# x copied into the output in DRAM, relu results added there by accumulating transfers, in a graph-attention layer kernel

## The reference

```python
h = jnp.maximum(_layernorm(x, axis=-1), 0.0)
q = jnp.einsum('c,bcn->bn', wq, h)
k = jnp.einsum('c,bcn->bn', wk, h)
scores = q[:, None, :] + k[:, :, None]
scores = jnp.where(scores > 0, scores, 0.01 * scores)
att = jax.nn.softmax(scores, axis=-1)
agg = jnp.einsum('bcn,bmn->bcm', h, att)
out = jnp.einsum('oc,bcm->bom', adj, agg) + bm[None, :, None]
x = x + jax.nn.relu(out)
```

## Time and profile before

| | us |
|---|---|
| median of 3 runs | 2090.09 |
| lowest, highest | 2087.72, 2090.14 |
| the profiled execution | 2090.47 |
| its span from first to last instruction | 2088.7 |
| PE busy | 2051.5 (98%) |
| DVE busy | 1674.8 (80%) |
| ACT busy | 1221.5 (58%) |
| POOL busy | 379.6 (18%) |
| DMA queue of SP, share of 16 engines | 37.1% |

### The profile page before, as it was taken

How to read it: one execution, slowest core, us unless ns; L and a number is a source line. 1 busy time by engine, 2 the same in 40 slices (tenths; PEclk the granted TensorE clock), 3 DMA queues, 4 the chain that set the end, 5 groups by cost and what they waited for, 6 DMA issues and landing times.

```text
span 2088.7 us, 33534 instructions
## 1 busy us (share of the span) xinstructions
PE 2051.5 (98%) x10448; PEld 950.3 (45%) x10448; DVE 1674.8 (80%) x3661; ACT 1221.5 (58%) x1871; POOL 379.6 (18%) x273
## 2 busy tenths in 40 slices
PE   5899999999999999999999999999999999999999
PEld 2344444444444444444444444444444444444444
DVE  7978878778887788887788877888877888778853
ACT  5556656556655566565566555665655665556634
POOL 1012211112111122111121111221111211112212
PEclk9999999999999999999999999999999999999999
DMA  5244433344324444333433234442334432343332
GB/s 195 64 155 142 148 99 123 138 160 141 133 84 136 151 141 146 104 118 137 161 141 133 84 136 151 141 146 105 117 137 161 141 131 86 136 152 141 106 101 76
DMA packets 126395, 271.46 MB, mean 130 GB/s; under 512 B 22624, under 2 KB 23136, under 8 KB 122208
## 3 DMA queue, kind: packets, MB, share of 16 engines
q1 hardware_dynamic: 123904, 269.01, 37.1%
q10 hardware_dynamic: 2400, 1.58, 0.3%
HBM read 202.91 MB, written 67.63 MB: 130 GB/s over the span
## 4 chain that ended last, share of the span: by engine, by line
PE 95%; DVE 3%; DMA 1%; POOL 0%; issue 0%; ACT 0%; POOLq 0%; SPq 0%; DVEq 0%
PE mix L385 21%; PE mix L387 21%; PE mix L386 21%; PE mix L362 10%; PE mix L363 10%; PE mix L364 10%; PE small L325 2%; DVE den_out L728 1%; PE small L334 1%; DMA xs<-in_x_dram 0%; DVE p_ring L749 0%; DVE p_lo L756 0%; DVE v_lo L761 0%; POOL wm_nat L893 0%; DMA den_row<-den_rows 0%
## 5 line engine op out<-in xcount | busy, mean ns | idle before, releaser
L385 PE MATMUL mix<-p_hi,v_hi 128*128 128x512 f16 x2048 | 776.3, 379 | 5.9 <-DVE p_lo L756 5.4
L386 PE MATMUL mix<-p_lo,v_hi 128*128 128x512 f16 x2048 | 776.2, 379 | 0.0
L387 PE MATMUL mix<-p_hi,v_lo 128*128 128x512 f16 x2048 | 776.2, 379 | 0.0
L911 POOL TENSOR_TENSOR res<-res,y 128x512 f32<-128x512 f32 x256 | 370.5, 1447 | 1688.2 <-ACT y L512 1688.2
L749 DVE SCALAR_TENSOR_TENSOR p_ring<-ab_row,cols,p_ring 128x512 f32<-128x512 f32 x512 | 377.1, 748 | 129.7 <-ACT p_ring L491 129.7
L491 ACT ACTIVATE p_ring<-ab_row,cols 128x512 f32<-128x512 f32 x512 | 349.5, 691 | 192.4 <-DMA ab_row<-ab_rows 132.3
L503 ACT ACTIVATE v_hi<-mix 128x512 f16<-128x512 f32 x256 | 152.7, 597 | 444.1 <-PE mix L364 443.5
L728 DVE SCALAR_TENSOR_TENSOR den_out<-den_row,cols 128x512 f32<-128x512 f32 x512 | 393.4, 806 | 1.0 <-DMA den_row<-den_rows 1.0
L362 PE MATMUL mix<-wmT_hi,h_hi 128*128 128x512 f16 x1024 | 389.1, 380 | 0.0
L364 PE MATMUL mix<-wmT_hi,h_lo 128*128 128x512 f16 x1024 | 388.8, 380 | 0.0
L363 PE MATMUL mix<-wmT_lo,h_hi 128*128 128x512 f16 x1024 | 388.8, 380 | 0.0
(11 more groups left out here) (71 smaller groups left out, 838.9 us busy)
## 6 DMA issues: line engine op xcount, KB each, us to landing
res<-in_x_dram SPq DMA_DIRECT2D x256, 256.0 KB, 3.2
out_dram<-res SPq DMA_DIRECT2D x256, 256.0 KB, 2.1
xs<-in_x_dram SPq DMA_DIRECT2D x124, 512.0 KB, 6.5
den_row<-den_rows SPq DMA_DIRECT2D x32, 1024.0 KB, 4.6
ab_row<-ab_rows SPq DMA_DIRECT2D x64, 512.0 KB, 5.0
res<-in_x_dram SPq DMA_DIRECT2D x4, 512.0 KB, 5.0
wm_nat<-in_adj_dram ACTq DMA_DIRECT2D x1, 1024.0 KB, 12.2
den_rows<-cols SPq DMA_DIRECT2D x32, 8.0 KB, 1.6
```

The costliest lines, as they stand in the source:

```text
L385: pe.matmul(ps[:, :], v_hi[:, b[1], nt, chans], p_hi[:, hf, nt, :], start=(nt == 0), stop=False)
L386: pe.matmul(ps[:, :], v_hi[:, b[1], nt, chans], p_lo[:, hf, nt, :], start=False, stop=False)
L387: mm = pe.matmul(ps[:, :], v_lo[:, b[1], nt, chans], p_hi[:, hf, nt, :], start=False, stop=(nt == NT - 1))
L911: pool.tensor_tensor(res[:, k, :], res[:, k, :], y[:, k % 2, :], ALU.add).then_inc(s_add, 1)
```

## The change

The tile res and its loads and stores are gone. Instead SP copies the whole x of a batch, 2 MB, into the output inside DRAM, by one transfer (copy_x). y now has eight slots, one for each unit. POOL no longer adds: for each unit it issues a transfer that adds y[k] to the output tile in DRAM (accum_op). For unit 0 it waits for the copy of that batch (s_xc). relu(b, k) on ACT now waits until the accumulating transfer of the same k of the batch before has landed (s_st[k]). On SP the transfers of the row scales, of xs, and of the exponentials stay in their sequence, with the copy of the next batch between xs and the exponentials. At the start x of the second batch lies in y, and scrap_wqk has a tile of its own.

```diff
-        y = sb("y", [P, 2, HALF])
-        res = sb("res", [P, U, HALF])
+        y = sb("y", [P, U, HALF])
...
-        x_second = res[:, :, :].rearrange("p (c h) n -> p c (h n)", h=2)
+        x_second = y[:, :, :].rearrange("p (c h) n -> p c (h n)", h=2)
-        scrap_wqk = y
+        scrap_wqk = sb("scrap_wqk", [P, 2, C])
...
-            def load_residual(b, k):
-                wait(sp, s_st[k], cnt(b, 16, 0))
-                sp.dma_start(res[:, k, :], tile_of(x, b, k)).then_inc(s_xr[k], 16)
-
-            def store(b, k):
-                sp.wait_ge(s_add, cnt(b, U, k + 1))
-                sp.dma_start(tile_of(out, b, k), res[:, k, :]).then_inc(s_st[k], 16)
+            def copy_x(b):
+                sp.dma_start(out[b[0] * 2 + b[1]], x[b[0] * 2 + b[1]]).then_inc(s_xc, 16)
...
-            for k in range(U):
-                sp.wait_ge(s_h32, CT + k // 2 + 1)
-                load_residual(first, k)
+            copy_x(first)
...
             def period(b, one, two, three):
-                store(b, 0)
-                for k in range(1, U):
-                    if one and k == 4:
-                        write_ab_rows(nxt(b))
-                        load_ab_rows(nxt(b))
-                    store(b, k)
-                    if one:
-                        load_residual(nxt(b), k - 1)
-                    if three and k == 4:
-                        for c in range(CT):
-                            load_x(nxt(b, 3), c)
                 if one:
-                    load_residual(nxt(b), U - 1)
+                    write_ab_rows(nxt(b))
+                    load_ab_rows(nxt(b))
+                if three:
+                    for c in range(CT):
+                        load_x(nxt(b, 3), c)
+                if one:
+                    copy_x(nxt(b))
                 if two:
                     write_den_rows(nxt(b, 2))
                     load_den_rows(nxt(b, 2))
...
-                wait(act, s_add, cnt(b, U, k - 1))
-                act.activation(y[:, k % 2, :], mix[k % MIX][:, :], ACT.Relu, bias=bias_o[:, ot:ot + 1],
+                wait(act, s_st[k], cnt(b, 16, 0))
+                act.activation(y[:, k, :], mix[k % MIX][:, :], ACT.Relu, bias=bias_o[:, ot:ot + 1],
                                scale=unscale_o[:, ot:ot + 1]).then_inc(s_y[k % 2], 1)
...
             def finish(b, k):
-                pool.wait_ge(s_xr[k], cnt(b, 16, 16))
+                hf, ot = divmod(k, OT)
+                tile = out[b[0] * 2 + b[1], ot * P:(ot + 1) * P, hf * HALF:(hf + 1) * HALF]
+                if k == 0:
+                    pool.wait_ge(s_xc, cnt(b, 16, 16))
                 pool.wait_ge(s_y[k % 2], cnt(b, U // 2, k // 2 + 1))
-                pool.tensor_tensor(res[:, k, :], res[:, k, :], y[:, k % 2, :], ALU.add).then_inc(s_add, 1)
+                pool.dma_start(tile, y[:, k, :], accum_op=ALU.add).then_inc(s_st[k], 16)
```

More of the change, by code:

```diff
@@ L142, in gnn_layer @@
         s_x1 = [sem(f"x1_loaded_{c}") for c in range(CT)]
-        s_xr = [sem(f"x_residual_loaded_{k}") for k in range(U)]
+        s_xc = sem("x_copied_to_out")
         s_id = sem("identity_ready")
@@ L180, in gnn_layer @@
         s_y = [sem(f"relu_done_{i}") for i in range(2)]
-        s_add = sem("unit_finished")
-        s_st = [sem(f"stored_{k}") for k in range(U)]
+        s_st = [sem(f"added_to_out_{k}") for k in range(U)]
         def nxt(b, by=1):
@@ L220, in load_x @@
                 sp.dma_start(xs[:, c, :], channels(b, c)).then_inc(s_x[c], 16)
-            def tile_of(tensor, b, k):
-                hf, ot = divmod(k, OT)
-                return tensor[b[0] * 2 + b[1], ot * P:(ot + 1) * P, hf * HALF:(hf + 1) * HALF]
-            def load_residual(b, k):
-                wait(sp, s_st[k], cnt(b, 16, 0))
-                sp.dma_start(res[:, k, :], tile_of(x, b, k)).then_inc(s_xr[k], 16)
-            def store(b, k):
-                sp.wait_ge(s_add, cnt(b, U, k + 1))
-                sp.dma_start(tile_of(out, b, k), res[:, k, :]).then_inc(s_st[k], 16)
+            def copy_x(b):
+                sp.dma_start(out[b[0] * 2 + b[1]], x[b[0] * 2 + b[1]]).then_inc(s_xc, 16)
             def write_den_rows(b):
```

## The result

The changed kernel takes 2092.39 us (median of 14 runs, 2088.5 to 2093.87). The kernel before takes 2088.44 us beside it (14 runs, 2087.29 to 2090.14). The ratio is 1.0016, with an interval of 1.0008 to 1.0023. So the change costs 3 to 4 us: the medians differ by 3.95, the ratio gives 3.3. Both lie within the 0.2%, 4.2 us, that the prediction called no change, but the interval's upper end, 4.8 us, does not. The predicted 2090.1 is 2.3 us low, inside the range of 2087.0 to 2098.0. The profiled execution took 2092.48 us, and its span is 2090.8.

A forecast was written before the change was run, and what follows sets the result against it. PE was taken to bound the kernel, busy 98% of the span and without gaps in a steady period. Start -1.1, body 0 and end +1.1 sum to 0, so 2090.1 us was forecast, range 2087.0 to 2098.0.

The forecast's parts named there:

- Start, -1.1: First 111 us or so: without POOL's addition DVE's L728 is 1.08 us shorter and PE starts earlier; -1.1 us.
- Copy, 0 at the start and 0 in the body: Copy of x inside DRAM, in the start and each period: done before anybody waits for what follows; 0.
- Row scales, 0 on a cover of 2.3 us: Each period: unit 4's accumulating tile delays the row-scale load by at most 1.3 us, under PE's 2.3 us cover; 0.
- Rival A: Body: unit 4's tile delays ab_row by 3.7 us, PE stands 1.4 us each period; 43 us, 2133; chance 0.10.
- Exponentials and den_row, 0: Each period: exponentials queue behind the copy but fit, and den_row has 4.5 us of cover; 0.
- ACT's new wait, 0: Body, relu on ACT: waits for a transfer issued some 63 us before, so it should have landed; 0.
- End, +1.1: Last relu to span end: 0.14 + 4.5 to landing + 0.37 = 5.0 us against 3.90; +1.1 us.
- B: Body: issuing on POOL stops DVE, and 2.0 us reach PE each period; 62 us, 2152; chance 0.04.
- C: Body: the copy is slow, at 25 us 4 us are missing each period; 124 us, 2214; chance 0.04.
- D: Body: accumulating tiles need over 8 us each and relu waits; at 9 us, 254 us, 2344; chance 0.03.
- E: Faster: freed time reaches PE and closes its 4.9 us of gaps between 60 and 110 us; 2085.2; chance 0.03.

The follow-up runs named there:

- before_trimmed: Kernel before, with POOL's third addition of the first batch held until DVE finished p, and DVE adding the very last unit; 2089.95 us, ratio 1.0001.
- copy_alone: Kernel before, plus the copy of each batch of x inside DRAM into scratch, issued on SP as in the changed kernel; 2089.48 us, ratio 1.0006.
- sw_store: Kernel before, with its additions kept but its stores issued by POOL as plain transfers, no accumulation; 2091.03 us, ratio 1.0011.
- tiny_1: Kernel before, plus one 8 KB transfer issued by POOL at the very start; 2090.52 us, one run.
- tiny_8: Kernel before, plus eight 8 KB transfers issued by POOL at the very start, each on its own semaphore; 2089.89 us, one run.

## Why the prediction was right, and where its steps were not

The time was in the range and the sign in the likeliest class. But the sum of 0 was reached with two terms too low, which gives +2.3 in place of 0: -1.1 + 1.0 + 2.4. Over the 2088.44 us measured beside it that is 1.0011, inside the measured 1.0008 to 1.0023. The call of no change held by a narrow margin. And by the prediction's own sign, wrong if a period differs from 63.83 us by over 0.13, its body was wrong: of 29 periods those of 63.97 and 64.04 differ by more, and one of the pair that takes 128.18.

- *Start, -1.1: right, and for its reason.* DVE's instruction is back at 0.74 us and the gap closed. Of the kernels in which that addition is replaced by a transfer or held by a wait, none has the gap. The changed kernel and those built on it have transfers; before_trimmed has the wait. Of those in which POOL adds there (before, copy_alone, sw_store, tiny_1, tiny_8), each has it, 1.0 us. The Trainium skill, "SBUF — State Buffer", section "Who interferes with whom", only infers that writing descriptors doesn't hold up such a DVE instruction. The trace agrees: 0.86 us of it begin inside L710, and L710 never exceeds 0.752 us. That the whole start is 1.29 us shorter proves less: the starts of the profiled executions scatter from 123.3 to 127.6 us, also between kernels that don't differ there (127.60 in the kernel before, 126.69 in tiny_8).
- *Copy, 0 at the start and 0 in the body: right.* "15 if the copy counts double" was too dear; it counts once.
- *Row scales, 0 on a cover of 2.3 us: this step failed, by 1.0 us in all.* Its upper bound was "at twice the cost 1.3 us". An accumulating byte costs 2.6 times a plain one, which is 1.8 us, and the trace shows 1.9 more between issue and ACT. A mean delay under the cover isn't enough either. Landings run from 4.1 to 8.1 us, and those beyond the cover reach PE. The step also put relu 4 at its old place. It now ends 19.7 us ahead of PE's product and not 18.2, since ACT waits less for DVE's low part (2.11 us, 3.58 before). So POOL issues the tile 0.4 us ahead of ab_row, with all of it in ab_row's way. The store that it replaces came 2.2 us behind the load, which the prediction left out. Rival A had the right mechanism at the right place, and its sign (an ACT wait for ab_row above 5 us) is in the trace; its 43 us assumed a delay of 3.7 us in every period.
- *Exponentials and den_row, 0: right.* den_row lands after 4.3/4.7/5.2 us, and DVE waits for it once, 0.8 us.
- *ACT's new wait, 0: right.* The slowest accumulating tile took 11.7 us of some 63 allowed.
- *End, +1.1: the mechanism was right, the term was mis-sized; it is +2.4.* 4.5 us from issue to landing was above the 3.9 measured, and POOL starts 0.30 us after relu, not 0.14. What failed is the 0.37 us behind the landing, which was carried over from SP's stores: it is 2.06, of which POOL's DRAIN takes 1.85. The estimate by the Trainium skill ("DMA: Bandwidth & Descriptors", "Anatomy of one DMA — SWDGE (gpsimd) path"), 2.6 us to landing and -0.8 for the term, is refuted by 3.9 us for an accumulating tile; sw_store's plain tiles, 2.5 us, agree with it.
- *Rivals B, C, D, E.* No L710 is longer beside an issue. DVE waits for den_row in the start alone (1.0 us before the change). ACT never waits for a tile added to the output, and no other PE gap near the start is gone. The argument against B, "of three additions only one cost DVE anything", was a little off: beside the addition that comes next, the short L735 took 0.62 us, and it takes 0.15 in the changed kernel, which is 15 of the 45 us that DVE lost.

## What to carry over

Taking work from an engine that nobody waits for gave nothing by itself; look for the one instruction that it disturbs, and for what the new traffic shares with the transfer that has the least cover. A transfer that accumulates in DRAM, of tiles like these, should be counted at 2.6 times its bytes and kept out of the window just ahead of a load on whose landing the bound engine depends, if need be by waiting for that landing. Leave the last unit to the engine and the queue with the shortest path to the end, and when POOL has issued hundreds of transfers, let it finish its part early: its DRAIN is covered then. Before moving one instruction, look also at the stores and refills that follow it: in before_trimmed they took back what the move gave.

## What the hardware showed that was not expected

- Accumulating into DRAM costs 1.76 us of all 16 engines for 256 KB, 149 GB/s; storing the same bytes 0.68 us, 387 GB/s; copying inside DRAM goes at 412 GB/s.
- After hundreds of transfers issued by POOL the program ends later: 2.06 us (accumulating) and 2.2 us (plain stores) from the last landing to the end of the span, where 0.4 to 0.5 is usual. The time is in POOL's DRAIN at the end, which grows with the transfers and with the semaphores that they use (0.07 us behind POOL's last instruction with none, 1.32 with 248 on one, 3.04 with 248 on eight). It costs nothing once POOL ends early.
- The start varies by itself. PE's products come every 0.43 us until 34.7 us in the profile of before and every 0.22 us from some 30 us on in the one after. In the one after the granted clock falls later on, after PE has been idle from 51.0 to 53.9 us: it is 0.50, the 1.2 GHz level, from 54 to 58 us, and products then come every 0.43 us. Window 50 to 60 us, before, then after:

```profile
50.00:60.00 10.00, 7.22 (x64) 3.64 (x63) 10.00 (x22) 3.29 (x5) 0.00 (x0) 1.00 0.49 162
```
```profile
50.00:60.00 10.00, 7.10 (x48) 2.95 (x47) 9.42 (x22) 1.21 (x3) 0.00 (x0) 0.66 0.00 0
```

The clock's level thus changes at other moments from one execution to the next. That this makes the scatter of the starts, and part of the 3 to 5 us that runs of one kernel span, is likely but wasn't tested.
